# First attention: the first of two units turned in two row halves of 64 queries

## What is computed

```
q = (x @ Wq.T + bq).reshape(B, S, H, HD).transpose(0, 2, 1, 3)
k = (x @ Wk.T + bk)...   # 8 heads, each used by 8 query heads
v = (x @ Wv.T + bv)...
scores = jnp.einsum('bhqd,bhkd->bhqk', q, k) * scale
allowed = (qi >= kj) & (qi - kj < WINDOW)
scores = jnp.where(allowed[None, None], scores, neg)
logits = jnp.concatenate([scores, sink], axis=-1)
probs = jax.nn.softmax(logits, axis=-1)[..., :-1]
o = jnp.einsum('bhqk,bhkd->bhqd', probs, v)
return o.transpose(0, 2, 1, 3).reshape(B, S, H * HD) @ Wo.T + bo
```

## Time and profile before

| | before |
|---|---|
| median of 3 runs | 3868.59 us (3867.06 to 3871.04) |
| the profiled execution | 3861.37 us |
| its span, first to last instruction | 3859.6 us |
| PE busy in the span | 3530.1 us (91%) |
| DVE busy | 3056.9 us (79%) |
| ACT busy | 2232.7 us (58%) |
| POOL busy | 1442.2 us (37%) |
| mean granted PE clock | 0.947 |

### The profile page before, as it was taken

How to read it: one execution, slowest core, us unless ns; L and a number is a source line. 1 busy time by engine, 2 the same in 40 slices (tenths; PEclk the granted TensorE clock), 3 DMA queues, 4 the chain that set the end, 5 groups by cost and what they waited for, 6 DMA issues and landing times.

```text
span 3859.6 us, 93855 instructions
## 1 busy us (share of the span) xinstructions
PE 3530.1 (91%) x32894; PEld 2461.0 (64%) x32894; DVE 3056.9 (79%) x11272; ACT 2232.7 (58%) x6991; POOL 1442.2 (37%) x1741
## 2 busy tenths in 40 slices
PE   7999999999999989999989969989878999899855
PEld 6888888888888866666644433335555666555532
DVE  7888888888888866677779967767886777888771
ACT  5888888888888842257654434433333222467611
POOL 2554554554554510145448855520000000222117
PEclk9999999999999989889989989999988999899958
DMA  3000000000000012210000000000000000000023
GB/s 130 3 3 3 3 3 3 3 3 3 3 3 3 3 53 85 71 67 2 2 1 1 0 11 0 1 1 1 1 1 34 1 1 1 34 2 2 23 61 49
DMA packets 30897, 64.58 MB, mean 17 GB/s; under 512 B 3424, under 2 KB 19808, under 8 KB 29152
## 3 DMA queue, kind: packets, MB, share of 16 engines
q1 hardware_dynamic: 24288, 52.29, 3.9%
q0 software_dynamic: 6144, 6.30, 1.0%
HBM read 49.93 MB, written 8.65 MB: 15 GB/s over the span
## 4 chain that ended last, share of the span: by engine, by line
PE 69%; DVE 17%; ACT 5%; issue 5%; POOL 2%; DMA 1%; DVEq 0%; POOLq 0%; ACTq 0%; SPq 0%
PE ps L176 9%; PE ps L537 8%; PE ps L497 7%; PE ps L473 6%; PE ps L521 6%; PE ps L1680 3%; PE ps L1651 3%; PE ps L1649 3%; PE ps L2304 3%; PE ps L2291 2%; DVE gbbc L2343 2%; PE ps L1020 2%; DVE gbbc L2332 2%; DVE gbbc L2338 2%; PE ps L998 2%
## 5 line engine op out<-in xcount | busy, mean ns | idle before, releaser
L742 ACT ACTIVATE T<-T 128x128 f32<-128x128 f32 x1024 | 397.3, 399 | 9.0 <-DVE T L663 9.0
L742 ACT ACTIVATE W<-T 128x128 f32<-128x128 f32 x1024 | 397.1, 399 | 1.3 <-DVE T L663 1.3
L643 DVE CUSTOM_DVE_ANT_0 T<-ps,C 128x128 f32<-128x128 f32 x1536 | 381.3, 286 | 0.0
L653 DVE COPY_PREDICATED W<-gbbc,ps 128x512 f32<-128x512 int32 x512 | 342.8, 722 | 3.2 <-PE ps L176 2.6
L537 PE MATMUL ps<-W,gbbc 64*64 64x128 f32 (+1 forms) x6912 | 319.6, 310 | 2.1 <-DVE W L653 1.2
L497 PE MATMUL ps<-T 64*64 64x192 f32 (+2 forms) x8192 | 317.2, 292 | 4.2 <-DVE T L643 4.2
L497 PEld LDWEIGHTS ps<-T 64*64 64x64 f32 x8192 | 254.3, 133 | 83.3 <-issue 45.2
L176 PE MATMUL ps<-C,T 128*128 128x128 f32 (+1 forms) x1620 | 260.6, 297 | 50.4 <-DVE T L307 19.1
L1247 POOL TENSOR_TENSOR QK<-T,QK 128x512 fp32r<-128x512 f32 x128 | 161.9, 1275 | 376.1 <-ACT T L1207 259.2
L537 PEld LDWEIGHTS ps<-W,gbbc 64*64 64x64 f32 x6912 | 280.1, 132 | 28.3 <-PE ps L537 23.1
L833 POOL TENSOR_TENSOR W<-W,T 128x512 f32<-128x512 f32 x256 | 260.8, 1040 | 77.9 <-DVE T L670 77.9
(11 more groups left out here) (420 smaller groups left out, 8803.2 us busy)
## 6 DMA issues: line engine op xcount, KB each, us to landing
T<-crow_dram SPq DMA_DIRECT2D x128, 128.0 KB, 3.0
W<-in_l1f_dram SPq DMA_DIRECT2D x1, 6152.0 KB, 18.3
W<-in_l0a_dram SPq DMA_DIRECT2D x1, 5172.5 KB, 25.5
W<-in_l2f_dram SPq DMA_DIRECT2D x1, 3160.0 KB, 10.8
W<-in_l3f_dram SPq DMA_DIRECT2D x1, 3076.0 KB, 10.0
W<-in_sm_dram SPq DMA_DIRECT2D x1, 2729.0 KB, 9.1
W<-in_l0f_dram SPq DMA_DIRECT2D x1, 2256.0 KB, 30.4
X<-in_x_dram SPq DMA_DIRECT2D x1, 2048.0 KB, 7.4
```

Of the source, the lines that this page charges most:

```text
L643: done(e.tensor_tensor_reduce(sm[:, at:at + 128], src, m, 1.0, -3.0e38, ALU.add, ALU.max, mx[:, col:col + 1]), s["masked"], x == (3 if ban ...
L653: e.copy_predicated(a.PT[t % 2][:, 512 + 512 * j:1024 + 512 * j].rearrange("p (h w) -> p h w", h=4), is_.unsqueeze(1).broadcast_to([P, 4, ...
L742: done(e.activation(a.Pr[i % 4][:, at:at + w_], a.Sm[i % 2][:, at:at + w_], ACT.Exp, bias=a.ngs[i % 4][:, c:c + 1], scale=a.scale, accum_o ...
```

## The change

The even unit's turn becomes `turn_crossed`. Each 128x128 transpose is cut into two, one for queries 0 to 63 (the upper row half of the array) and one for queries 64 to 127 (the lower), each with 128 columns of weights and 64 columns of identity, 16 in all. The two halves of the array work on different banks at any time: in step 0 the first half writes bank c=0 and the second c=1, in step 1 the other way round. Between the steps PE waits on its own last matmul of step 0, on a new count `crossed` (on a semaphore that a later stage uses as `max`). All waits for other engines stand ahead of the first matmul, and `parted` of the even unit waits for the full count. The odd unit's turn stays as it was.

```diff
-    a.s |= again(k, "soft", summed=("gather", u), beats=("sel", 2 * a.groups), ebbs=("mT", 2 * a.groups))
+    a.s |= again(k, "soft", summed=("gather", u), beats=("sel", 2 * a.groups), ebbs=("mT", 2 * a.groups), crossed=("max", u // 2))
...
+    def turn_crossed(i):
+        e.wait_ge(*s["norm"](2 * i + 2))
+        past(e, s["o"], i - 1)
+        past(e, s["even"], i)
+        for step in range(2):
+            if step:
+                e.wait_ge(*s["crossed"](i // 2 + 1))
+            for h in range(4):
+                for r in range(2):
+                    c, rows = r ^ step, slice(64 * r, 64 * r + 64)
+                    at, q = 512 * c + 128 * h, 128 * h + 64 * r
+                    m = e.transpose(a.Tb[i % 2][c][:, q:q + 64], a.Pr[i % 4][rows, at:at + 128], k.C["ident"][rows, rows])
+                    done(m, s["turn"], step == 1 and h == 3)
+                    done(m, s["crossed"], step == 0 and h == 3 and r == 1)
...
     def turn(i):
         for c in range(2):
             e.wait_ge(*s["norm"](2 * i + c + 1))
-            if c == 0 and i % 2 == 0:
-                past(e, s["even"], i)
-            elif c == 0 or i % 2 == 0:
+            if c == 0:
                 past(e, s["o"], i - 1)
...
         if turning is not None:
-            turn(2 * turning)
+            turn_crossed(2 * turning)
...
     def parted(t):
         bank = a.Tb[t % 2][0]
-        e.wait_ge(*s["turn"](2 * t + 1))
+        e.wait_ge(*s["turn"](2 * t + 2 - t % 2))
```

## The result

| | before | changed |
|---|---|---|
| median, first measurement | 3867.8 us (3866.6 to 3871.0, 4 runs) | 3891.8 us (3882.2 to 3898.7, 4 runs) |
| ratio, 95% interval | | 1.0049 (1.0026 to 1.0073) |
| profiled execution, span | 3861.4, 3859.6 us | 3888.4, 3886.6 us |

The change made the kernel slower, by 19 us by the ratio, with an interval from 10 to 28. The forecast was 3880.0, 11.4 us slower, in a range of 3867 to 3892; the measured median lies at the upper edge of that range, and two of its four runs, 3895.2 and 3898.7, lie above it.

A forecast was written before the change was run, and what follows sets the result against it. PE was taken to bound the first attention's rounds; 0.10 us more at each even turn x 128 gave +12.8 us, less a part at batch boundaries +11.4, added to the median 3868.6: 3880.0 us, range 3867 to 3892.

The forecast's parts named there:

- What bounds: First attention: PE bounds each 10.27 us round, so what it gains or loses at the even turn moves the round.
- Pace: Even turn: one pair of half-array transposes every 0.055 us, with 0.06 as the other bound.
- rival 2: Even turn: PE's wait or pace is costlier, 0.14 to 0.20 us per round, 3886 to 3894 us; chance 0.08.
- The wait: Between the even turn's two steps: released weight load begins 0.095 us after the record's end; PE stands for 0.31 us.
- The exit: From even turn to q0 projection (L473): a change of tiles, records 0.145 us apart, then 0.11 us of open weights.
- Rival 4: Leaving the even turn is free, L473's weights load under the last pairs: -0.10 us per round, 3856 us; chance 0.06.
- The entry: From 64*64 scores into the 64*128 even turn: gap stays at its present 0.16 us; other bound zero gap.
- rival 1: From scores into the even turn the change of tiles is free: near nothing, 3868 to 3871 us; chance 0.12.
- Other edits at zero: Even turn's earlier waits for other engines and DVE's later masked copy: nothing late, zero; 0 to 0.05 us allowed.
- The part given back: Rounds at a batch's boundary, DVE late: slower PE costs nothing there; at most 3 us of 12.8, half taken.
- Sum and total: First attention: 0.10 us more per round x 128 = +12.8 us, taken as +11.4 us; whole kernel 3880.0 us.
- The up to 2x: Even turn at the skill page's speedup: 0.43 us less per round, 55 us in all, 3813 us; chance 0.01.

The follow-up runs named there:

- no-wait kernel: Changed kernel without PE's wait between the steps, each half keeping its bank (output not the reference's): 3851.3 us, ratio 0.9940 to the kernel before.
- both-crossed kernel: Changed kernel with the odd unit's turn cut into row halves in the same way too: 3931.8 us, one run.

## Why the prediction came out as it did

- **What bounds.** Right. The chain stays on PE, and the 0.09 us at the even turn and the projection behind it moved the round by 0.09; DVE and ACT waited longer for it. That the round falls by 0.28 when the wait goes shows the same downward.
- **Pace.** Forecast 0.055 from the columns, with 0.06 as the other bound. It was 0.06 to 0.062, in the no-wait kernel's seven paces and in the changed kernel's last pairs: the bound of rival 2, which so came true in this part. It is near the 0.06 of open load in the earlier trace rows, so the weights' side may set it; no run shows which side does. Six paces, 0.04 us too little.
- **The wait.** Forecast 0.095 from the record's end to the released load, taken from the values. It was 0.06 (median of 128 by the records), 0.035 too much. The two errors cancel, so that the turn came out at 0.92, as in the sum, is luck. As a price against running on, the wait measured 0.28 when it went and 0.27 to 0.28 for a second one. The sum itself has 0.32 for it: the last record of step 1 begins at 0.775, and seven paces from 0.06 on would put it at 0.45. The 0.255 of my expectations took a pace of 0.055 off the 0.31, though that pace was already in it (0.285 is where the next pair would stream), so it came near by a second slip.
- **The exit.** Right: the first record of L473 is 0.48 long with 0.10 of open weights (0.11 forecast), and it begins 0.15 behind the last of the turn (0.145 forecast), a gap of 0.09 over the pace, as the earlier trace rows had it. The chain's 1.06 against 0.86 is this term as a row. Rival 4 falls by it.
- **The entry.** Taken as unchanged. The last score's record and the turn's first stand 0.156 us apart in the changed kernel and before, so rival 1 falls: 64*64 to 64*128 costs what 64*64 to 128*128 did. The rule of the Trainium skill, page "TensorEngine Tiling (Array Packing)", section "Tiling Modes", says that a change of mode drains TensorE. The traces agree where I had no row (0.156 as before) and on the way in and out of the row halves in the both-crossed kernel (0.09 of gap each way).
- **Other edits at zero.** Right: ratio 1.0004, the even turn 1.03.
- **The part given back.** Wrong: 1.4 us were taken off for the rounds behind a batch's boundary, where DVE was thought to be late. Nothing was given back. These rounds grew from 10.50 to 10.59 and from 10.41 to 10.50 us, by 0.09 as an ordinary one (10.28 to 10.37), and their chain stays on PE. DVE bounds them only in the both-crossed kernel, where they grew by more.
- **Sum and total.** 11.4 us forecast, 12 measured in the rounds. This nearness is luck again: 0.10 a round was 0.09 (12.8 us were 12), and the 1.4 given back was nothing. The measured median is 24 us higher, the ratio 19. What lies beyond the rounds I had left out, the scatter of the clock above all: I took the three runs of before, 4 us apart, for the scatter of the kernel, and over all later executions of that same kernel it was 3861 to 3893. The range was wide enough for other reasons than the one needed. How much of what lies beyond the rounds, 7 us by the ratio and 12 by the medians, is scatter and how much belongs to the change stays open.
- **The up to 2x.** The Trainium skill, page "TensorEngine Tiling (Array Packing)", section "Overview", gives up to 2x for a contraction of 64 or less. Of that the pace has 1.8x (0.109 against 0.062 us for one head's 128 columns), and sixteen matmuls without the wait have 0.65 us in the chain, in place of 0.87 or 1.03. With the wait and the exit nothing of it was left in the round.

## What to carry to other kernels

Halving a matmul's columns by working in row halves pays only for a stretch that is long against its fixed costs: a change of tiles at each end that was not there before (here 0.09 us and the first open weights of 0.06 to 0.11) and 0.27 to 0.28 us for each time that PE waits for its own last matmul before the halves swap banks. With 8 transposes of 0.109 us there were 0.43 us to win and 0.52 to pay (wait 0.28, exit 0.19, and 0.05 because the pace was 0.062 and not 0.055). Before cutting so, list these gaps, and look for other work of the same tiles to put into the wait (not tried here); check that no other engine's copy moves behind the longer turn, as in the both-crossed kernel; and measure a change of a few tenths of a percent by its rounds in the trace, since the total scatters by more than that.

## What was not expected of the hardware

- The time from the end of a matmul's record to the weight load that it releases depended on the tiles: 0.06 us in row halves (64*128, 64 moving columns), 0.09 in 64*64 tiles with 128 moving columns, 0.12 in the whole array (the chain has 0.04, none and 0.14 as a piece called issue). The ends of these records are modelled, so the difference may be in the model; from the start of the last matmul to the released load it was 0.28 in the row halves, 0.36 in the values and 0.39 in the whole array.
- In the first attention's first 50 us, the same program had mean clocks of 0.66 and 0.76, and between kernels that do not differ there before 58 us they went from 0.66 to 0.90. The clock then stayed at 1.00 up to the end of the stage, with the new turn as with the old.
